# Cross-attention and feed-forward, one core: x loaded ahead of the high halves' transposition, its statistics in two parts

## The chip, the core and the metric

The kernel runs on one core of a Trainium2 chip. The metric is the device time of one execution in microseconds (us), the median of several runs. The core has a matrix engine (TensorE, PE in the profile), VectorE (DVE), ScalarE (ACT), GpSimd (POOL) and SyncE (SP), which here issues every DMA. The engines run their own instruction lists in order and meet at semaphores: an instruction whose semaphore has not reached its value holds everything behind it on its engine. That holds for SyncE too: a DMA that waits keeps back all DMAs behind it.

## What is computed

A block of 16 batches with 512 tokens of width 512: attention over 120 context rows with rotary positions (16 heads of 32), and a gated feed-forward (512 to 1536 to 512) whose tensors are quantised and dequantised by their largest value.

```
x = x + xattn(layernorm(x), ctx, ctx, Wq, Wk, Wv, Wo)
x = x + ffn(layernorm(x), w_gate, w_up, w_down)

# xattn: rope on q and k, softmax of q k^T / sqrt(32), times v, times Wo
# ffn:   x, up, gate, gate*sigmoid(gate) and the product are rounded to
#        16 bit levels of their largest value, weights to 4 bit in blocks of 32
```

## The kernel before

It has four stages one after the other: attention for all batches (to about 740 us), then the gate, the up and the down projection, each bound by TensorE. Only the attention stage is touched.

**Steps.** Attention is cut into units, one per batch and quarter of the heads: 4 x 16 = 64 units `u`. A loop over steps `s` (0 to 66) is written out on each engine (`sp_attention`, `pe_attention`, `act_attention`, `dve_attention`, `pool_attention`), with `b, c = divmod(s, 4)`, and each step works on several units at different depths. In a middle step TensorE does, in this order: the scores of unit s-7 (line 668, then the maxima's part, 675), the queries of unit s (693), the scores from which the row maxima are taken, of unit s-2 (716), the output projection of an old unit (752), every fourth step (c = 2) the transposition of the maxima (726), and the values and sums of unit s-7 (771, 776). All scores use the same four banks of PSUM, so the scores of line 668 wait for VectorE's maxima (line 1341) of the step before, and the scores of line 716 wait for ScalarE's exponentials (line 975).

**Queries.** ScalarE copies the queries of unit s out of PSUM (998). The rotation needs neighbouring rows swapped: SyncE does this with two DMAs (`sp_swap`, lines 398 and 399, tile QW). GpSimd multiplies with the cosine (1471) and, when the swap has landed, the sine (1480); VectorE adds the two in the next step (`dve_rope_add`, 1139), ahead of the maxima of unit s-2 on its list.

**x of a batch.** One tile X (XA[0]) holds x of one batch at a time. Which step does what for batch nb is set by `x_at(s, part)`, which is true for s = 4 nb - 5 + part (for nb from 3 on):
- `sp_x_load` (424): 1 MB from memory into X, in step 4 nb - 6 (c = 2), behind the transposition of the batch before. It waits for s_xlo, that is until VectorE has computed the low halves of the batch before out of X.
- `dve_x_stats` (1149, 1154), step 4 nb - 5 (c = 3): four sums (BN_STATS) and their means, at the end of the step's list. GpSimd makes the deviations from them (`pool_deviation`, 1488 and 1490, a power), VectorE the shift (`dve_x_shift`, 1160) and ScalarE the normalised x (933), step 4 nb - 4 (c = 0).
- `act_x_high` and `dve_x_low` (946, 1169), step 4 nb - 3 (c = 1): x is split into a high and a low half of 16 bit (ST).
- `sp_x_turn` (433): each half is transposed by a DMA into XD, the high one in step 4 nb - 3 (c = 1), the low one in the next (c = 2). The queries of batch nb begin in step 4 nb.

So in a step with c = 1 SyncE issues the high transposition of batch nb, in the next the low one and then the load of batch nb + 1.

**Also in the row.** On SyncE stand in every step the write of x1 (x plus attention) of one unit (465), the load of its next x row (480), and the two swaps; in c = 0 and 1 two loads each of reciprocal rows (445, tile RB) which GpSimd multiplies into the attention output (1505) before ScalarE's copies (1018); in c = 3 the sums are written out and read back (451, 455), in c = 0 the reciprocals go out (459). VectorE begins each step with x1 of a unit and its statistics (1191, 1203, 1208, 1209), and every fourth step has a part of the feed-forward weights' preparation (1244 to 1264).

Of the kernel before, what the change touches and what calls it, by code (L numbers as in the profile page):

```python
# [13 lines left out]
B, S, D, NH, SK, F = 16, 512, 512, 16, 120, 1536  # L14
# [31 lines left out]
def kv_at(s):  # L46

    first = sum(n for t, n in KV_STEPS.items() if t < s)
    return range(first, first + KV_STEPS.get(s, 0))
# [16 lines left out]
def normal_at(s):  # L66

    b, c = divmod(s - 13, 4)
    return [4 * b + 2 * c, 4 * b + 2 * c + 1] if 0 <= b < B - 2 and c < 2 else []


def output_at(s):

    if s < 16:
        return []
    return [s - 16] if s < NU + 1 else [[LATE - 1, LATE], [LATE + 1], [LATE + 2]][s - NU - 1]
# [7 lines left out]
def x_at(s, part):  # L84

    for b in range(2, B):
        if s == 4 * b - 5 + part + (b == 2):
            return [b]
    return []


def w_step(k):

    return 16 + 4 * k


def build(nc, x, ctxt, wq, wk, wv, wo, w_gate, w_up, w_down, cosq, sinq, cosk, sink, eye, out, scr):
    x1_d, g_d, gq_d, up_d, xt_d, wt_d, sr_d = scr
    stack = ExitStack()
    with stack:  # L100
# [269 lines left out]
        def w_home(k):  # L370
            return wt_d[k // 12, k % 12]

        def x1_rows(b):
            return x[b].rearrange("(p j) d -> p j d", j=4)
# [18 lines left out]
        def sp_swap(e, n, w):  # L393

            e.wait_ge(s_qe, n + 1)
            if n >= 2:
                e.wait_ge(s_radd, n - 1)
            e.dma_start(QW[n % 2][0:128:2, 0:w], qe(n)[1:128:2, 0:w]).then_inc(s_qw[n % 2], 16)
            e.dma_start(QW[n % 2][1:128:2, 0:w], qe(n)[0:128:2, 0:w]).then_inc(s_qw[n % 2], 16)

        def sp_ctx_load(e, g):
            if g == 1:
                e.wait_ge(s_clo, 1)
            elif g == 2:
                e.wait_ge(s_wlo, 1)
            elif g == 3:
                e.wait_ge(s_am, AMAX.index("ctx1") + 1)
                e.wait_ge(s_tp, 4)
            e.dma_start(CX[g][0:SK], ctxt[4 * g:4 * g + 4].rearrange("b s d -> s b d")).then_inc(CXS[g][0], 16)
# [11 lines left out]
        def sp_x_load(e, b):  # L421
            if b:
                e.wait_ge(s_xlo, 2 * b)
            e.dma_start(X[:], x1_rows(b)).then_inc(s_x, 16)
# [32 lines left out]
        def dma_recip_out(e, b):  # L457
            e.wait_ge(s_rr, rr(b))
            e.dma_start(sr_d[1 + b % 2].rearrange("r (e f) -> (r e) f", f=64), RG[:]).then_inc(s_rd, 16)

        def sp_x1_out(e, u):

            _, x1, i, _ = x_of(u)
            e.wait_ge(s_x1, u + 1)
            e.dma_start(x1_d[u // 4, :, u % 4, :], x1).then_inc(s_x1d[i], 16)
# [25 lines left out]
        def sp_attention(e):  # L491
            e.dma_start(id32[:], eye).then_inc(s_id, 16)
            sp_ctx_load(e, 0)
            e.dma_start(WLD[0], wk.rearrange("(k p) e -> p k e", p=128)).then_inc(s_wld[0], 16)
            sp_x_load(e, 0)
            for a, t in ((ck, cosk), (sk, sink)):
                e.dma_start(a, t).then_inc(s_tab, 16)
            e.dma_start(WLD[1], wq.rearrange("(k p) e -> p k e", p=128)).then_inc(s_wld[1], 16)
            for a, t in ((cq[:], cosq), (sq[:], sinq)):
                e.dma_start(a, t).then_inc(s_tab, 16)  # L500
            e.dma_start(WLD[2], wv.rearrange("(k p) e -> p k e", p=128)).then_inc(s_wld[2], 16)
            sp_ctx_load(e, 1)
            sp_ctx_load(e, 2)
            for n in range(4):
                sp_swap(e, n, 4 * SK)
            sp_x_load(e, 1)
            for s in range(NSTEP):
                b, c = divmod(s, 4)

                for u in output_at(s - 1):  # L510
                    sp_x1_out(e, u)
                for u in output_at(s + 1):
                    sp_xr_load(e, u)

                if c == 0 and 0 <= b - 3 < B - 1:
                    dma_recip_out(e, b - 3)
                if s < NU:
                    sp_swap(e, ROT["q", s], 512)
                for i in kv_at(s):
                    if i % 8 < 4:  # L520
                        sp_swap(e, ROT["k", i], 4 * SK)

                for u in normal_at(s + 1):
                    dma_recip(e, u)

                if c == 3 and 0 <= b - 2 < B - 1:
                    dma_sums_out(e, b - 2)
                    dma_sums_in(e, b - 2)
                if s == 1:
                    sp_ctx_load(e, 3)  # L530
                if s == 4:
                    sp_ctx_turn(e, 2)
                if s == 6:
                    sp_ctx_turn(e, 3)
                if s == 9:
                    e.wait_ge(s_v, 12)
                    e.dma_start(WLD[3], wo.rearrange("(k p) e -> p k e", p=128)).then_inc(s_wld[3], 16)

                for nb in [1] if s == 2 else x_at(s, 2):
                    sp_x_turn(e, nb, 0)  # L540
                    if s < 16:
                        sp_x_turn(e, nb, 1)
                for nb in x_at(s - 1, 2) if s > 16 else []:
                    sp_x_turn(e, nb, 1)
                if c == 2 and 2 <= b + 2 < B:
                    sp_x_load(e, b + 2)

                for k in range(12):
                    if w_step(k) == s:
                        if k == 0:  # L550
                            e.wait_ge(s_v, 16)
                        if k >= 2:
                            e.wait_ge(s_wl, k - 1)
                        e.dma_start(w_ld[k % 2], w_source(k)).then_inc(s_ld[k % 2], 16)
                    if w_step(k) + 6 == s:
                        e.wait_ge(s_wl, k + 1)
                        e.dma_start(w_home(k), w_hl).then_inc(s_ws, 16)
                if s >= 57:
                    sp_gate_turn(e, s - 57)

                if s == 64:
                    for i in range(2):
                        if i == 0:
                            e.wait_ge(s_xlo, 2 * B)
                        else:
                            e.wait_ge(s_xt, 32 * (B - 1))
                        e.wait_ge(s_x1d[0], 32 * (i + 1))
                        e.wait_ge(s_x1d[1], 32 * (i + 1))
                        e.dma_start(XA[i][:], x1_d[i]).then_inc(s_xl[i], 16)

            dma_sums_out(e, B - 2)
            sp_x1_out(e, LATE + 1)
            sp_xr_load(e, LATE + 3)
            sp_xr_load(e, LATE + 4)
            dma_sums_in(e, B - 2)
            sp_x1_out(e, LATE + 2)
            sp_xr_load(e, LATE + 5)
            dma_recip_out(e, B - 2)
            for u in range(NU - 8, NU - 4):
                dma_recip(e, u)  # L580
            sp_x1_out(e, LATE + 3)
            sp_xr_load(e, LATE + 6)
            for u in range(LATE + 4, NU):
                sp_x1_out(e, u)
                if u + 3 < NU:
                    sp_xr_load(e, u + 3)
                if u == NU - 4:
                    sp_gate_turn(e, NO - 2)
                    sp_gate_turn(e, NO - 1)
# [551 lines left out]
                g, r = divmod(i, 8)  # L1141
                e.tensor_tensor(KR[g][:, r, :], KR[g][:, r, :], QW[n % 2][:, 0:4 * SK], ALU.add).then_inc(s_radd, 1)

        def dve_x_stats(e, b):
            e.wait_ge(s_x, 16 * (b + 1))
            if b >= 2:
                e.wait_ge(s_lmv, b - 1)
            for j in range(4):
                e.bn_stats(st1[b % 2][:, j, :], X[:, j, :]).then_inc(s_lst, 1)
            e.wait_ge(s_lst, 4 * b + 4)  # L1150
            if b >= 2:
                e.wait_ge(s_lnb, b - 1)
            for j in range(4):
                t = e.bn_aggr(mv1[b % 2][:, j, :], st1[b % 2][:, j, :])
            t.then_inc(s_lmv, 1)

        def dve_x_shift(e, b):
            q = rs1[b % 2]
            e.wait_ge(s_lrs, 2 * b + 2)
            e.scalar_tensor_tensor(q[:, 4:8], mv1[b % 2][:, :, 0], -1.0, q[:, 0:4], ALU.mult, ALU.mult).then_inc(s_lnb, 1)  # L1160
# [105 lines left out]
        def dve_attention(e):  # L1266
# [35 lines left out]
            for s in range(NSTEP):  # L1302
                b, c = divmod(s, 4)
# [11 lines left out]
                    dve_x_stats(e, 1)  # L1315
                if s == 1:
                    dve_x_shift(e, 1)
                if 1 <= s <= NU:
                    dve_rope_add(e, ROT["q", s - 1])
                    for i in kv_at(s - 1):  # L1320
                        if i % 8 < 4:
                            dve_rope_add(e, ROT["k", i])
# [1083 lines left out]
```

## Time and profile before

| | us |
|---|---|
| median of 3 runs | 2319.28 (2317.97 to 2320.76) |
| profiled execution | 2318.47 |
| its span in the trace | 2316.7 |
| TensorE busy | 2199.2 (95%) |
| VectorE busy | 1686.2 (73%) |
| ScalarE busy | 1330.6 (57%) |
| GpSimd busy | 704.9 (30%) |

Shares of the whole span say little here, since attention and the feed-forward have different limits. From 400 to 500 us, in the middle of attention, TensorE is busy 94.2 us, VectorE 89.6, ScalarE 63.0 and GpSimd 69.7, the DMA engines at a share of 0.80, and TensorE's clock is granted in full. A step takes about 9 to 10 us, a batch about 38.

A row of a timeline gives the start in us, the time it took, engine, line, operation, the tiles it writes and reads, how many instructions were merged in it, and in brackets how long the engine was idle before it and what ended that. In steps 37 to 41 the first scores of TensorE (line 668) start at 433.71, 442.56, 452.59, 461.74 and 472.47; what VectorE does for a step runs a little behind that. Times in the text are those of this trace.

### The profile page before, as it was taken

What the parts mean: (1) busy time and instruction counts of PE and PEld (TensorE: products, weight loads), DVE (VectorE), ACT (ScalarE), POOL (GpSimd) and SP (SyncE); (2) the same over time, 40 slices, a digit from 0 to 9 for tenths busy, and PEclk for the clock granted to TensorE, in tenths of its full rate; (3) what the DMA queues carried; (4) which work ended last, traced back from release to release, by engine and by line L of the source; (5) the groups of instructions that cost most, each with busy time, mean ns of one, the idle gap of its engine ahead of it and who ended that gap; (6) DMA issues with size and microseconds to landing.
All of it is one profiled execution on the core that took longest, in us unless ns stands there. A gap on an engine that the chain in (4) does not pass through costs nothing. (4 is left out here: it accounts for less than half of the span.)

```text
span 2316.7 us, 31161 instructions
## 1 busy us (share of the span) xinstructions
PE 2199.2 (95%) x12037; PEld 970.5 (42%) x12037; DVE 1686.2 (73%) x1690; ACT 1330.6 (57%) x1299; POOL 704.9 (30%) x655
## 2 busy tenths in 40 slices
PE   5898999999988899999999999999998799999999
PEld 3443333333332444444444444444443344444444
DVE  7656899898975766445543598888888887778773
ACT  3345666666644232222322787877877777777772
POOL 3444675766663311000100364444444000000000
PEclk9899999999999999999999999999999899999999
DMA  6334686877777568888875898877876565655552
GB/s 193 95 103 116 179 194 173 193 173 192 170 159 178 164 215 256 272 246 253 250 227 180 292 329 311 299 286 286 293 284 259 189 234 211 236 226 205 205 217 91
DMA packets 287190, 500.14 MB, mean 216 GB/s; under 512 B 187980, under 2 KB 190284, under 8 KB 250172
## 3 DMA queue, kind: packets, MB, share of 16 engines
q1 hardware_dynamic: 287036, 498.10, 68.1%
q8 instruction: 95, 1.56, 0.3%
q14 instruction: 59, 0.48, 0.1%
HBM read 247.75 MB, written 186.58 MB: 187 GB/s over the span
## 5 line engine op out<-in xcount | busy, mean ns | idle before, releaser
L1698 PE MATMUL banks<-XB,W 128*128 128x512 f16 x2304 | 500.1, 380 | 2.3 <-ACT XB L1724 2.3
L1698 PE MATMUL banks<-XB,WT 128*128 128x512 f16 x2304 | 497.4, 379 | 0.0
L2164 PE MATMUL banks<-W,OH 128*128 128x512 f16 x2256 | 487.1, 379 | 3.6 <-DVE OH L2266 3.6
L1718 ACT ACTIVATE OB<-banks,uns 128x512 f32<-128x512 f32 x384 | 255.7, 684 | 393.2 <-PE banks L1698 390.4
L1698 PEld LDWEIGHTS banks<-XB,W 128*128 128x128 f16 x2304 | 225.9, 98 | 276.1 <-issue 5.1
L1698 PEld LDWEIGHTS banks<-XB,WT 128*128 128x128 f16 x2304 | 225.4, 98 | 271.8
L2164 PEld LDWEIGHTS banks<-W,OH 128*128 128x128 f16 x2256 | 220.7, 98 | 270.0 <-DVE OH L2266 4.0
L1985 POOL TENSOR_TENSOR PR<-GS,OB 128x2048 f32<-128x2048 f32 x46 | 220.5, 4794 | 257.6 <-ACT OB L1718 247.6
L1807 DVE TENSOR_REDUCE amx<-OB 128x1 f32<-128x2048 f32 x48 | 109.7, 2285 | 239.8 <-ACT OB L1718 239.8
L752 PE MATMUL banks<-XC,AH 128*128 128x512 f16 x768 | 179.2, 385 | 5.4 <-POOL AH L1510 3.7
L693 PE MATMUL banks<-XD,WQ 128*128 128x512 f16 x768 | 177.0, 380 | 2.2 <-ACT WQ L878 0.8
L975 ACT ACTIVATE P<-banks 120x2048 f32<-120x2048 f32 x60 | 112.3, 1872 | 86.5 <-PE banks L675 86.5
L1341 DVE TENSOR_REDUCE MX<-banks 128x16 f32<-128x1920 f32 x64 | 137.6, 2149 | 25.2 <-PE banks L716 25.2
L1949 DVE TENSOR_REDUCE amf<-PR 128x4 f32<-128x2048 f32 x47 | 107.4, 2286 | 52.5 <-POOL PR L1985 52.1
L2227 ACT ACTIVATE OH<-OQ 128x2048 f16<-128x2048 int16 x47 | 89.5, 1904 | 93.7 <-DVE OQ L2261 92.7
L2289 DVE SCALAR_TENSOR_TENSOR Y<-banks,gm,XRd 128x512 f32<-128x512 f32 x64 | 46.3, 745 | 116.5 <-PE banks L2164 116.5
L1480 POOL TENSOR_TENSOR QW<-QW,sq 128x512 f32<-128x512 f32 x64 | 90.3, 1411 | 130.6 <-DMA QW<-QE 129.9
L2247 DVE SCALAR_TENSOR_TENSOR GSd<-SQd,XD 128x2048 f32<-128x2048 int32 x47 | 107.6, 2289 | 15.2 <-ACT SQd L2209 15.2
L693 PEld LDWEIGHTS banks<-XD,WQ 128*128 128x128 f16 x768 | 70.1, 98 | 113.4 <-issue 33.6
L1931 DVE SCALAR_TENSOR_TENSOR GS<-SQ,GQ 128x2048 f32<-128x2048 int32 x48 | 109.5, 2282 | 9.8 <-ACT SQ L1906 9.8
L1933 DVE TENSOR_REDUCE amg<-GS 128x1 f32<-128x2048 f32 x48 | 109.7, 2286 | 1.7
L2261 DVE SCALAR_TENSOR_TENSOR OQ<-AQ,gm,BQ 128x2048 int16<-128x2048 int16 x47 | 110.1, 2342 | 0.9 <-ACT AQ L2215 0.9
(272 smaller groups left out, 2866.2 us busy)
## 6 DMA issues: line engine op xcount, KB each, us to landing
g_s<-OB SPq DMA_DIRECT2D x48, 1024.0 KB, 6.0
GL<-g_s SPq DMA_DIRECT2D x48, 1024.0 KB, 7.3
up_s<-OB SPq DMA_DIRECT2D x48, 1024.0 KB, 4.9
XA<-up_s SPq DMA_DIRECT2D x32, 1024.0 KB, 9.3
gq_s<-GQ SPq DMA_DIRECT2D x48, 512.0 KB, 4.7
XD<-gq_s SPq DMA_DIRECT2D x48, 512.0 KB, 6.7
XA<-in_x SPq DMA_DIRECT2D x16, 1024.0 KB, 6.3
QW<-QE SPq DMA_DIRECT2D x128, 128.0 KB, 3.0
```

The costliest lines, as they stand in the source:

```text
L693: t = e.matmul(BQ_.rearrange("p (j t) -> p j t", j=4), WQ[:, a, k, c * 128:(c + 1) * 128], XT[b % 2][:, xa, :, k, :], start=(n == 0 and k ...
L752: t = e.matmul(o_bank(u), AH[b % 2][:, a, k, j * 128:(j + 1) * 128], WO[:, wa, k, :], start=(n == 0), stop=(n == 11))
L975: e.activation(P[0:SK], PB[0:SK, 0:4, :], ACT.Exp, scale=SM_SCALE).then_inc(s_p, 1)
L1341: e.tensor_reduce(MX[mb % 2][:, :, :, mc].rearrange("p j g -> p g j"), PB[:, 0:4, 0:4 * SK].rearrange("p g (j s) -> p g j s", j=4), AX.X, ...
L1698: t = e.matmul(pk[:].rearrange("p (j t) -> p j t", j=4), WT[w][:, ot, wa, kk, :], XB[i % 2][:, xa, :, kk, :], start=(kk == 0 and wa == 0 a ...
L1718: e.activation(OB[n % 3][:, r, :], bank[(k + 4) % 8][:], ACT.Copy, scale=uns[:, 12 * w + ot:12 * w + ot + 1]).then_inc(s_ev, 1)
L1807: e.tensor_reduce(amx[:, m:m + 1], flat(OB[m % 3][:]), AX.X, ALU.max, apply_absolute_value=True).then_inc(s_gr, 1)
L1931: e.scalar_tensor_tensor(GS[m % 2][:], SQ[m % 2][:], 65535.0, GQ[m % 2][:], ALU.min, ALU.mult).then_inc(s_gs, 1)
L1933: e.tensor_reduce(amg[:, m:m + 1], GS[m % 2][:], AX.X, ALU.max, apply_absolute_value=True).then_inc(s_gsm, 1)
L1985: e.tensor_tensor(PR[:], GS[m % 2][:].rearrange("p (a t) -> p a t", a=4), OB[(NC + m) % 3][:], ALU.mult).then_inc(s_pr, 1)
L2164: t = e.matmul(pk[:].rearrange("p (r n) -> p r n", r=4), OH[i % 2][:, a, ot, j * 128:(j + 1) * 128], WD[:, :, c, wa, o4, :], start=(ot == ...
L2261: e.scalar_tensor_tensor(OQ[m % 2][:], AQ[m % 2][:], gm[:, 10:11], BQ[m % 2][:], ALU.mult, ALU.mult).then_inc(s_doq, 1)
```

## The change

On SyncE, from step 16 on, the load of x moves from step 4 nb - 6 (c = 2, behind the low halves' transposition of batch nb - 1) to step 4 nb - 7 (c = 1, ahead of its high halves' transposition). It concerns batches 6 to 15. Its wait for s_xlo is unchanged and now stands ahead of the transposition's waits.

On VectorE the function `dve_x_stats` is split. For batches 6 to 15 the sums of the first two quarters are taken by `dve_x_sums(e, nb, 0)` in the same step (c = 3), but behind x1's statistics and ahead of the addition on the queries; the other two sums and the means stay where all four were.

```
+                if s >= 16 and c == 1 and b + 2 < B:
+                    sp_x_load(e, b + 2)
                 for nb in [1] if s == 2 else x_at(s, 2):
                     sp_x_turn(e, nb, 0)
                     if s < 16:
                         sp_x_turn(e, nb, 1)
                 for nb in x_at(s - 1, 2) if s > 16 else []:
                     sp_x_turn(e, nb, 1)
-                if c == 2 and 2 <= b + 2 < B:
+                if s < 16 and c == 2:
                     sp_x_load(e, b + 2)
...
-        def dve_x_stats(e, b):
+        def dve_x_sums(e, b, part):
+
             e.wait_ge(s_x, 16 * (b + 1))
             if b >= 2:
                 e.wait_ge(s_lmv, b - 1)
-            for j in range(4):
+            for j in range(2 * part, 2 * part + 2):
                 e.bn_stats(st1[b % 2][:, j, :], X[:, j, :]).then_inc(s_lst, 1)
+
+        def dve_x_stats(e, b):
+            if b < 6:
+                dve_x_sums(e, b, 0)
+            dve_x_sums(e, b, 1)
             e.wait_ge(s_lst, 4 * b + 4)
...
                 if s == 1:
                     dve_x_shift(e, 1)
+                for nb in x_at(s, 0) if s >= 16 else []:
+                    dve_x_sums(e, nb, 0)
                 if 1 <= s <= NU:
                     dve_rope_add(e, ROT["q", s - 1])
```

SyncE in a step with c = 1 and the next, before (line 433 is a transposition, 465 x1 out, 480 an x row in, 398 and 399 the swap, 424 the load of x):

```order
185 L433 DMA_TRANSPOSE XD<-XA 128x16x128
186 L465 DMA x_s<-RX 128x512
187 L480 DMA RX<-in_x 128x512
188 L398 DMA QW<-QE 64x512
189 L399 DMA QW<-QE 64x512
190 L433 DMA_TRANSPOSE XD<-XA 128x16x128
191 L424 DMA XA<-in_x 128x2048
192 L557 DMA wt_s<-RW 128x1024
193 L465 DMA x_s<-RX 128x512
```

and after the change:

```order
185 L424 DMA XA<-in_x 128x2048
186 L433 DMA_TRANSPOSE XD<-XA 128x16x128
187 L465 DMA x_s<-RX 128x512
188 L480 DMA RX<-in_x 128x512
189 L398 DMA QW<-QE 64x512
190 L399 DMA QW<-QE 64x512
191 L433 DMA_TRANSPOSE XD<-XA 128x16x128
192 L559 DMA wt_s<-RW 128x1024
193 L465 DMA x_s<-RX 128x512
```

The load has moved past both transpositions, x1's two transfers and one swap.

VectorE in a step with c = 3, before (the row of x1's statistics, the addition on the queries, the maxima, the sums of x, their means, and x1 of the next step):

```order
150 L1209 TENSOR_REDUCE xmn<-RX 128x1
151 L1139 TENSOR_TENSOR QR<-QR,QW 128x512
152 L1341 TENSOR_REDUCE MX<-banks 128x4x4
153 L1149 BN_STATS st<-XA 128x6 x4
154 L1154 BN_AGGR mv<-st 128x2 x4
155 L1191 SCALAR_TENSOR_TENSOR RX<-banks,vun,RX 128x512
```

and after (lines 1141, 1351, 1152, 1162 and 1199 are what 1139, 1341, 1149, 1154 and 1191 were):

```order
150 L1217 TENSOR_REDUCE xmn<-RX 128x1
151 L1152 BN_STATS st<-XA 128x6 x2
152 L1141 TENSOR_TENSOR QR<-QR,QW 128x512
153 L1351 TENSOR_REDUCE MX<-banks 128x4x4
154 L1152 BN_STATS st<-XA 128x6 x2
155 L1162 BN_AGGR mv<-st 128x2 x4
```

Two of the four sums have moved ahead of the addition and the maxima; the rest keeps its order.

## Rows read from the trace of the kernel before

**Rows 1.** Waits of TensorE, 340 to 640: us in total, times, longest.

```profile
PE banks L668 <- DVE MX L1341: 10.1, 9, 1.8
PE banks L716 <- ACT P L975: 6.1, 12, 0.8
```

**Rows 2.** Timeline of TensorE, steps 37 to 41.

```profile
433.71 1.13 PE L668 MATMUL banks<-QR,W 32*120 32x512 f32 x8 [1.40 <-DVE MX L1341]
...
447.29 0.39 PE L716 MATMUL banks<-W,QE 32*128 32x120 f16 x16 [0.68 <-ACT P L975]
...
461.74 1.13 PE L668 MATMUL banks<-QR,W 32*120 32x512 f32 x8
...
465.72 0.39 PE L716 MATMUL banks<-W,QE 32*128 32x120 f16 x16
...
472.47 1.13 PE L668 MATMUL banks<-QR,W 32*120 32x512 f32 x8 [1.81 <-DVE MX L1341]
```

**Rows 3.** Timeline of VectorE, steps 39 and 40.

```profile
456.77 1.63 DVE L1139 TENSOR_TENSOR QR<-QR,QW 128x512 f32<-128x512 f32 x1 [0.94 <-POOL QW L1480]
458.32 2.15 DVE L1341 TENSOR_REDUCE MX<-banks 128x16 f32<-128x1920 f32 x1
462.19 2.47 DVE L1149 BATCH_NORM_STATS2 st<-XA 128x6 f32<-128x512 f32 x4 [1.72 <-DMA XA<-in_x]
...
470.27 2.14 DVE L1341 TENSOR_REDUCE MX<-banks 128x16 f32<-128x1920 f32 x1
```

**Rows 4.** Timeline of SyncE, steps 36 to 40.

```profile
433.23 1.25 SPq L445 DMA_DIRECT2D RB<-sr_s  x2
...
444.81 5.20 SPq L433 DMA_TRANSPOSE XD<-XA  x1
...
451.22 0.53 SPq L398 DMA_DIRECT2D QW<-QE  x1
...
455.51 0.85 SPq L424 DMA_DIRECT2D XA<-in_x  x1
...
470.33 1.25 SPq L445 DMA_DIRECT2D RB<-sr_s  x2
```

**Rows 5.** DMA issues, 340 to 640: count, KB each, median us from issue to landing.

```profile
XA<-in_x SPq DMA_DIRECT2D x8, 1024.0 KB, 6.4
```

**Rows 6.** DMA issues, about 451.8: the swap of step 38.

```profile
QW<-QE SPq DMA_DIRECT2D x2, 128.0 KB, 3.5
```

**Rows 7.** DMA issues, about 459.1: the swap of step 39.

```profile
QW<-QE SPq DMA_DIRECT2D x2, 128.0 KB, 6.4
```

**Rows 8.** DMA issues, 444.5 to 445.5: the high halves' transposition, us to landing.

```profile
XD<-XA SPq DMA_TRANSPOSE x1, 8.0
```

**Rows 9.** Timeline of GpSimd, steps 38 and 39.

```profile
455.47 1.27 POOL L1480 TENSOR_TENSOR QW<-QW,sq 128x512 f32<-128x512 f32 x1
...
466.13 1.27 POOL L1480 TENSOR_TENSOR QW<-QW,sq 128x512 f32<-128x512 f32 x1 [5.47 <-DMA QW<-QE]
...
467.76 1.32 POOL L1490 TENSOR_TENSOR rs<-rs,mh 128x4 f32<-128x4 f32 x1
```

**Rows 10.** Timelines of TensorE, VectorE and SyncE in an early batch, step 17.

```profile
247.14 1.13 PE L668 MATMUL banks<-QR,W 32*120 32x512 f32 x8
...
254.01 4.30 DVE L1169 TENSOR_TENSOR XA<-XA 128x1024 f16<-128x1024 f32 x2 [0.30 <-ACT XA L946]
...
255.74 5.77 SPq L433 DMA_TRANSPOSE XD<-XA  x1
...
262.70 0.52 SPq L398 DMA_DIRECT2D QW<-QE  x1
```

**Rows 11.** Stretches: their length, busy us of each engine, clock, DMA share, GB/s.

```profile
444.00:446.00 2.00, 2.00 (x10) 0.88 (x9) 1.52 (x3) 1.88 (x3) 2.00 (x3) 1.00 0.27 99
446.00:448.00 2.00, 1.32 (x21) 0.56 (x20) 1.42 (x1) 1.28 (x2) 2.00 (x3) 1.00 2.01 151
...
457.00:462.00 5.00, 5.00 (x48) 1.86 (x44) 3.47 (x2) 2.08 (x5) 3.66 (x3) 1.00 0.91 262
```

More of the change, by code:

```diff
@@ L537, in sp_attention @@
                     e.dma_start(WLD[3], wo.rearrange("(k p) e -> p k e", p=128)).then_inc(s_wld[3], 16)
+                if s >= 16 and c == 1 and b + 2 < B:
+                    sp_x_load(e, b + 2)
                 for nb in [1] if s == 2 else x_at(s, 2):
@@ L544, in sp_attention @@
                     sp_x_turn(e, nb, 1)
-                if c == 2 and 2 <= b + 2 < B:
+                if s < 16 and c == 2:
                     sp_x_load(e, b + 2)
@@ L1142, in dve_rope_add, with dve_x_sums @@
                 e.tensor_tensor(KR[g][:, r, :], KR[g][:, r, :], QW[n % 2][:, 0:4 * SK], ALU.add).then_inc(s_radd, 1)
-        def dve_x_stats(e, b):
+        def dve_x_sums(e, b, part):
             e.wait_ge(s_x, 16 * (b + 1))
@@ L1147, in dve_x_stats @@
                 e.wait_ge(s_lmv, b - 1)
-            for j in range(4):
+            for j in range(2 * part, 2 * part + 2):
                 e.bn_stats(st1[b % 2][:, j, :], X[:, j, :]).then_inc(s_lst, 1)
+        def dve_x_stats(e, b):
+            if b < 6:
+                dve_x_sums(e, b, 0)
+            dve_x_sums(e, b, 1)
             e.wait_ge(s_lst, 4 * b + 4)
@@ L1317, in dve_attention @@
                     dve_x_shift(e, 1)
+                for nb in x_at(s, 0) if s >= 16 else []:
+                    dve_x_sums(e, nb, 0)
                 if 1 <= s <= NU:
```

## The prediction, made before the changed kernel ran

> **What bounds the kernel now.** I read the views in the order of the groups. First the waits of TensorE between 340 and 640 us: nearly all its holes are 10.1 us before the scores, on the score maxima of VectorE (9 times), and 6.1 us on the exponentials of ScalarE (12 times) [rows 1]. So this stretch is bound by TensorE with some 16 us of holes, and the change can't give more than that. Its timeline shows where the first kind lies: the scores of step 41 start at 472.47 after 1.81 us of waiting, those of step 37 at 433.71 after 1.40, those of step 40 at 461.74 without [rows 2]. Eight of the nine are in steps with s mod 4 = 1, once a batch; the first two of the ten batches that the change touches have none. The ninth is a short one, and I leave it in.
>
> Next, who makes VectorE late there. Its timeline in steps 39 and 40: it ends the maxima of step 39 at 460.47, stands idle 1.72 us until x has landed, takes the four sums from 462.19 to 464.66, then the means, x1 with its statistics, the addition on the queries, reciprocal and shift, and only at 470.27 the maxima of step 40 [rows 3], though TensorE had written their scores at 466.11 [rows 2]. Behind that lies the queue of SyncE: x is issued at 455.51 [rows 4] and takes 6.4 us in the median to land [rows 5]. The swap of the queries behind it takes 6.4 us too, where that of the step before took 3.5 [rows 6, 7]. GpSimd therefore stands idle 5.47 us before the sine product of step 39 [rows 9].
>
> **The change part by part.** The work is the same: four sums of 2.47/4 = 0.62 us, one x load and two transpositions a batch. Batches 6 to 15 are touched, ten in all, and only places change.
>
> The load goes from behind the low halves' transposition (step 38) to before the high halves' (step 37), some ten us earlier: the 1.72 us of waiting go. Two of the sums (1.24 us) go ahead of the addition on the queries, where VectorE was idle 0.94 us from 455.83 on [rows 3]: that addition starts at 455.83 + 1.24 = 457.07, 0.30 late. The maxima of step 39 end at 460.77, the other two sums at 462.0 instead of 464.66: 2.7 us earlier. The swap of step 39 has no load ahead of it; issued at 459.1 and given the 3.5 us of rows 6, it lands at 462.6, the sine product (1.27 us) ends near 463.9, the power for the deviations (1.32 us) near 465.5 [rows 9]. So GpSimd does not hold VectorE there, and its maxima of step 40, 2.7 us ahead at most, wait for the scores at 466.11: they run from some 467.6 at the latest to 469.7. TensorE wants them at 470.66 (472.47 less 1.81). The wait goes: **-10.1 us**, bounds 0 and -10.1.
>
> What is late next is the swap of step 38, behind the load, the high transposition, x1 and its x row. It landed at 451.8 + 3.5 = 455.3 [rows 6], just when GpSimd was free for it (sine product at 455.47 [rows 9]). VectorE's addition waits for that product; the maxima behind it end at 460.47 and TensorE wants them at 461.74 [rows 2, 3]: 1.27 us of slack, of which the sums take 0.30, so 1.0 is left. How late will the swap be? Issuing the load takes 0.6 of SyncE (0.59 in most of its rows; the one shown has 0.85 [rows 4]). For the load's bytes the trace has no plain load ahead of a transposition here. While SyncE issues the transposition (5.20 us [rows 4]) the engines move 99 GB/s at a busy share of 0.27; under the load they move 262 [rows 11]. If it fits into that gap, (262 - 99) GB/s x 5.2 us = 0.85 of its 1.05 MB go there, and 0.20 MB, 0.8 us, are left. If nothing fits, as the busy share of 2.01 from 446 to 448 [rows 11] may mean, it costs 1.05 MB / 262 GB/s = 4.0 us. I take 0.8, as SyncE's 5.2 us of issuing look like what sets the pace: delay 1.4 us, of which 0.4 reaches TensorE, ten times: **+4.0 us**; bounds 0 and 10 x (4.6 - 1.0) = +36.
>
> The Trainium skill speaks against this choice: Advanced Engine Details and Errata, section X-Bar Transpose (TRN2), says that transposing transfers run as fast as regular ones. There would be no gap then, the load would push the swap by its full 4.0 us and the sum would be a loss. The trace disagrees so far: 512 KB of transposition take 8.0 us to land, 1024 KB of load 6.4 [rows 5, 8].
>
> The load also waits for the low halves of the batch before (s_xlo), and behind it on SyncE stand the transposition and the swap. In the early batch VectorE computes the low halves until 254.01 + 4.30 = 258.31 and SyncE is ready at 255.74: 2.57 us of new waiting [rows 10]; in 5 of the ten batches SyncE comes first in this way. There, however, the swap was issued 15.6 us behind the scores of the step before (262.70 - 247.14 [rows 10], the scores of step 17 and the swap of step 18), against 451.22 - 433.71 = 17.5 around 444 [rows 2, 4], so such a batch only gets to where the others are. I price it at nothing; bound 1 us for each of the five. The transposed halves are wanted in step 40 only, x1's rows a step later: over 5 us of cover.
>
> Last, the waits on the exponentials. At 447.29 TensorE waits 0.68 [rows 2] since ScalarE's copies wait for GpSimd's product, and that for the reciprocals' rows, issued at 433.23 [rows 4], 0.48 us before the scores of step 37. Where they were issued 2.14 ahead (470.33 against 472.47 [rows 2, 4]) this wait is absent. Five of the 12 are of this kind, 3.4 us. With reciprocal and swap 2 us earlier the rows go out near 468.2, 2.4 us ahead of 470.66: these waits should go. I count half, **-1.7 us**, bounds 0 and -6.1.
>
> Sum: -10.1 + 4.0 - 1.7 = -7.8 us. The profiled execution took 2318.47 (span 2316.7, 1.8 around it) and becomes 2310.7; the median of the runs is 0.8 higher, so 2319.28 - 7.8 = **2311.5 us**. Everything behind 740 us is the same instructions.
>
> **The rivals.** *The collision only moves* (2319). The wait of step 41 goes and one as long comes at the scores of step 40. For it: the swap of step 38 has no slack at GpSimd, and the load waits in half of the batches. Against: the 99 GB/s under the transposition. With the swap 2.2 us late, 10 x (2.2 - 1.0) = 12 us eat the 11.8 gained.
>
> *Slower* (2328). Same place, one mechanism: the load's bytes do not fit into the transposition, and the swap of step 38 lands 3 us or more late. Price: 10 x (3.0 - 1.0) - 11.8 = +8.2, so 2327.5; it decides from 2.2 us of delay on. Rows 6 and 7 show the mechanism at today's place, 2.9 us between a swap behind the load and one that is not. The first two batches, with no wait to win, pay first. The Trainium skill, DMA: Bandwidth & Descriptors, section Queues, rings and completion order, has each engine take its descriptors in ring order; by that rule every byte of the load stands before the swap.
>
> *All holes close* (2303). The swap is late by under 1 us and both kinds of wait go: -10.1 - 6.1 = -16.2. For it: the first two batches run without the first kind. Against: the maxima of step 39 keep but 1.0 us of slack.
>
> **How the numbers follow.** Forecast 2311.5 (its own range 2307 to 2316): 0.45. Moved collision: 0.25. Slower: 0.18. All holes: 0.12. The range leaves out the upper half of the slower case and the end of the last: 2303.0 to 2325.0. About 0.2%, 4.6 us, is what a measurement of this kernel can tell from no change. Faster (below 2314.6) takes the first case but for its edge and the last: 0.54; same 0.27; slower (above 2323.9) 0.19.
>
> **What would show it.** Right: no idle VectorE before the sums, no wait at the scores of s mod 4 = 1; the swap of s mod 4 = 3 landing in about 3.5 us, and GpSimd's 5.47 us of idling gone; at s mod 4 = 0 waits of 0 to 0.6 us. Wrong: TensorE waiting 1 us or more on the maxima at s mod 4 = 0, GpSimd idle before the sine product of s mod 4 = 2, SyncE standing at the load for the low halves with everything behind it late. If TensorE's holes hardly shrink though the wait for x is gone, the error is in the 0.8 us.

## The result, and the profile after

| | before | after |
|---|---|---|
| median of 9 runs each | 2319.28 us (2316.29 to 2326.7) | 2331.57 us (2325.08 to 2334.59) |
| profiled execution | 2318.47 | 2331.95 |
| its span | 2316.7 | 2330.1 |

The changed kernel takes 1.0046 times as long, 95% interval 1.0032 to 1.006. That is 12.3 us more, where 7.8 less was forecast; the time lies above the range as well. The sign and the place are those of the rival called *Slower*, and the loss is larger than its 8.2 us. Some kernels of the experiments had one execution that was far longer than the rest (2381 to 11083 us); the ratios leave it out, the medians count it, which moves them by up to 1.3 us.

First the waits of TensorE after the change, 340 to 640 us (us in total, times, longest); they answer to [rows 1].

```profile
PE banks L670 <- DVE MX L1351: 13.5, 8, 3.0
PE banks L718 <- ACT P L977: 5.4, 9, 0.8
```

The wait for the score maxima has grown from 10.1 to 13.5 us. Its place has changed completely: over 240 to 640 there are ten such waits, 17.6 us, and all ten are at the scores of steps with s mod 4 = 0, one a batch; at s mod 4 = 1 there is none left. The timeline of TensorE in the batch with one of the largest, steps s mod 4 = 3, 0 and 1:

```profile
421.39 1.13 PE L670 MATMUL banks<-QR,W 32*120 32x512 f32 x8
...
433.49 2.08 PE L670 MATMUL banks<-QR,W 32*120 32x512 f32 x8 [2.88 <-DVE MX L1351]
...
443.83 1.14 PE L670 MATMUL banks<-QR,W 32*120 32x512 f32 x8
```

Who is late? VectorE, the same stretch; the row with 3.92 is the addition on the queries, and the first row the two sums that the change moved:

```profile
424.54 1.28 DVE L1152 BATCH_NORM_STATS2 st<-XA 128x6 f32<-128x512 f32 x2
429.73 1.63 DVE L1141 TENSOR_TENSOR QR<-QR,QW 128x512 f32<-128x512 f32 x1 [3.92 <-POOL QW L1490]
431.28 2.15 DVE L1351 TENSOR_REDUCE MX<-banks 128x16 f32<-128x1920 f32 x1
433.35 1.27 DVE L1152 BATCH_NORM_STATS2 st<-XA 128x6 f32<-128x512 f32 x2
```

The sums no longer wait for x: the 1.72 us of [rows 3] are gone. But the addition waits 3.92 us for GpSimd's sine product, where it waited 0.94. GpSimd in turn waited for the swap, and the swap of the next step arrives promptly:

```profile
428.42 1.28 POOL L1490 TENSOR_TENSOR QW<-QW,sq 128x512 f32<-128x512 f32 x1 [4.21 <-DMA QW<-QE]
...
434.33 1.27 POOL L1490 TENSOR_TENSOR QW<-QW,sq 128x512 f32<-128x512 f32 x1 [0.74 <-DMA QW<-QE]
```

And behind the swap lies SyncE, from the load of x on (step s mod 4 = 1) to the swap of step s mod 4 = 3:

```profile
413.59 0.47 SPq L424 DMA_DIRECT2D XA<-in_x  x1
414.17 8.30 SPq L433 DMA_TRANSPOSE XD<-XA  x1
...
423.66 0.52 SPq L398 DMA_DIRECT2D QW<-QE  x1
424.23 1.12 SPq L399 DMA_DIRECT2D QW<-QE  x1
425.45 3.12 SPq L433 DMA_TRANSPOSE XD<-XA  x1
...
430.78 0.62 SPq L399 DMA_DIRECT2D QW<-QE  x1
```

This is the row to look at. SyncE stands at the high transposition for 8.30 us, against 5.20 in [rows 4]. Everything behind it on SyncE is late by that, and so is the swap, whose own transfer has not become slower: the DMA issues around 413.6 to 414.5 and at 423.7 (us to landing) show it.

```profile
XA<-in_x SPq DMA_DIRECT2D x1, 1024.0 KB, 9.3
...
XD<-XA SPq DMA_TRANSPOSE x1, 11.9
```

```profile
QW<-QE SPq DMA_DIRECT2D x2, 128.0 KB, 3.6
```

**All ten batches.** I took the same instants in each, counted from the scores of the step with s mod 4 = 1 (the means of ten, 240 to 660 us; the trace of each kernel's profiled execution):

| us | before | after |
|---|---|---|
| high transposition starts on SyncE | 10.0 | 11.1 |
| SyncE stands at it | 5.5 | 7.6 |
| swap of s mod 4 = 2 has landed | 21.45 | 24.3 |
| scores of s mod 4 = 0 | 27.8 | 29.4 |
| from there to the next s mod 4 = 1 | 10.0 | 9.65 |
| whole batch | 37.8 | 39.1 |

Ten batches are 12.8 us longer, which is the loss within its noise. It is +16.3 up to the scores of s mod 4 = 0 and -3.5 behind them. Behind the landing stand the sine product 1.28, the addition 1.63 and the maxima 2.15, 5.1 us together; 24.3 + 5.1 = 29.4, so after the change this chain ends last in the mean of the batches. Before, 21.45 + 5.1 = 26.6 left 1.2 us of slack. The delay is 2.85 us, and 10 x (2.85 - 1.2) = 16.5.

### The profile page after: what moved, and what is told of

Its sections match the earlier page's. It is cut to its first block and busy times, and to the rows that moved or that the text cites. A ratio compares the mean times of both kernels' runs of the same rounds, so it can differ in the third digit from the quotient of the medians.

```text
span 2330.1 us, 31175 instructions
## 1 busy us (share of the span) xinstructions
PE 2206.6 (95%) x12037; PEld 972.2 (42%) x12037; DVE 1679.0 (72%) x1690; ACT 1328.1 (57%) x1299; POOL 704.1 (30%) x655
## 5 line engine op out<-in xcount | busy, mean ns | idle before, releaser
L695 PE MATMUL banks<-XD,WQ 128*128 128x512 f16 x768 | 182.0, 388 | 2.3 <-ACT WQ L880 0.8
```

The source lines that it names most:

```text
L695: t = e.matmul(BQ_.rearrange("p (j t) -> p j t", j=4), WQ[:, a, k, c * 128:(c + 1) * 128], XT[b % 2][:, xa, :, k, :], start=(n == 0 and k ...
```

## The experiments

Each edit is against the changed kernel, except where it is said; ratios are to the kernel before. "Stands at it" is SyncE's time at the high transposition and "landed" the instant of the table above, both as means of ten batches.

### The four sums left together

If the split of the sums were to blame, leaving them together would bring the time back. The load is moved as in the change; the sums stand where they were.

```
         def dve_x_stats(e, b):
-            if b < 6:
-                dve_x_sums(e, b, 0)
+            dve_x_sums(e, b, 0)
             dve_x_sums(e, b, 1)
...
-                for nb in x_at(s, 0) if s >= 16 else []:
-                    dve_x_sums(e, nb, 0)
```

> Only the load of x is moved ahead of the high halves' transposition; the four sums stay together behind the maxima. Theory 1 (the load's bytes hold up the transposition, SyncE stays 8 us instead of 5 in its issue, and the swap of s mod 4 = 2 lands some 4 us late): as slow as the whole change, ratio to before 1.003 to 1.008, waits of TensorE at the scores of s mod 4 = 0 still 1 to 3 us in most batches, since the two sums lay in VectorE's idle time. Theory 2 (the two sums ahead of the addition on the queries make the maxima late): ratio 0.997 or less, and waits at s mod 4 = 0 under 0.5 us.

Measured: 2330.82 us, ratio 1.0055 (1.004 to 1.0071). The split is not to blame; the moved load alone makes the loss.

### The same instructions with fewer bytes

The rest of the change is kept, with its wait for the low halves, but the load of batches 6 to 15 brings a quarter or a half of x, so that the other parts of the tile keep old values.

```
-            e.dma_start(X[:], x1_rows(b)).then_inc(s_x, 16)
+            if b >= 6:
+                e.dma_start(X[:, 0:1, :], x1_rows(b)[:, 0:1, :]).then_inc(s_x, 16)
+            else:
+                e.dma_start(X[:], x1_rows(b)).then_inc(s_x, 16)
```

> The change with a load that brings only one of four parts of x for batches 6 to 15 (256 KB instead of 1024; the other three parts keep old values, so this leaves out three quarters of the loads). Place, issue and the wait for the low halves are unchanged. Theory 1 (bytes): the transposition's issue goes back to about 5 us, the swap of s mod 4 = 2 is late by 1 to 2 us, TensorE's waits at s mod 4 = 0 fall from 17.6 us in all to under 6, ratio to before 0.994 to 0.998. Theory 3 (SyncE standing at the load for the low halves, 10.2 us in all, makes the swap late): waits stay at 10 us or more, ratio 1.001 or more.

The half (`0:2` in place of `0:1`):

> The change with a load of only the first two of four parts (512 KB; leaves out half of x for batches 6 to 15). It sets the dose between 256 KB (ratio 0.994) and 1024 KB (1.005). If the delay of the swap grows with the bytes and only what exceeds about 1 us of slack reaches TensorE: swap 1.5 to 2.5 us late, waits at s mod 4 = 0 between 2 and 9 us in all, ratio 0.996 to 1.000. If there is a fixed cost of any larger load there, 1.003 or more.

Measured, with the changed kernel beside them:

| load | time us | ratio | landed |
|---|---|---|---|
| 256 KB | 2304.23 | 0.9944 (0.993 to 0.9957) | 21.4 |
| 512 KB | 2307.78 | 0.9959 (0.9944 to 0.9973) | 22.3 |
| 1024 KB, the change | 2331.57 | 1.0046 (1.0032 to 1.006) | 24.3 |

SyncE with 256 KB, the rows that answer to 413.59 to 424.23 above:

```profile
402.00 0.34 SPq L425 DMA_DIRECT2D XA<-in_x  x1
402.44 5.07 SPq L436 DMA_TRANSPOSE XD<-XA  x1
...
408.71 0.52 SPq L398 DMA_DIRECT2D QW<-QE  x1
```

With a quarter of the bytes SyncE stands at the transposition for 4.7 us in the mean, with all of them 7.6: 2.9 more, and the swap lands 2.9 later. In both the transposition starts 11.1 us behind the scores, so the load's place, its issue and its wait for the low halves are the same, and in the kernel with 256 KB they cost nothing: its swap lands at 21.4, as before the change. SyncE does wait for the low halves, eight times in the changed kernel (the line below, 240 to 640 us), and nine times, 14.7 us, in this one, which is the fastest of all:

```profile
SPq L424 <- DVE XA L1177: 10.2, 8, 2.7
```

TensorE's wait for the maxima is as good as gone with 256 KB (240 to 640):

```profile
PE banks L721 <- ACT P L980: 4.0, 7, 0.8
PE banks L673 <- DVE MX L1354: 0.2, 1, 0.2
```

So the bytes ahead of the transposition are what makes the swap late. From 256 to 1024 KB are 0.79 MB, and at the 262 GB/s of [rows 11] that is 3.0 us; the landing moves by 2.9. So each byte beyond the first quarter is paid in full, as if nothing of it went under the transposition. The time follows with a threshold, since up to 1.2 us of delay there is slack: 22.3 is still within it, 24.3 is not. These two kernels also move less in all; the next ones don't.

### The same bytes behind the high transposition

The load is issued in the same step, directly behind the transposition instead of ahead of it.

```
-                if s >= 16 and c == 1 and b + 2 < B:
-                    sp_x_load(e, b + 2)
                 for nb in [1] if s == 2 else x_at(s, 2):
                     sp_x_turn(e, nb, 0)
                     if s < 16:
                         sp_x_turn(e, nb, 1)
+                if s >= 16 and c == 1 and b + 2 < B:
+                    sp_x_load(e, b + 2)
```

> The change, but with the load issued directly behind the high halves' transposition instead of ahead of it, still ahead of x1's two transfers and the swap of s mod 4 = 2. Theory A (bytes simply add: whatever stands ahead of the swap delays it by 1 MB / 262 GB/s = 4 us): same as the change, ratio 1.003 to 1.007, waits at s mod 4 = 0 of 14 to 20 us in all. Theory B (a load ahead of a transposition is worse than one behind it, since the transposition's issue on SyncE then grows from 5 to 8 us and holds all that is behind): the issue is back at 5 us, the swap is issued 3 us earlier, and the ratio is 0.997 to 1.002.

Measured: 2316.45 us, ratio 0.9992 (0.9981 to 1.0002), no difference to the kernel before. SyncE in one batch:

```profile
410.64 5.05 SPq L433 DMA_TRANSPOSE XD<-XA  x1
415.73 0.57 SPq L424 DMA_DIRECT2D XA<-in_x  x1
...
418.59 0.59 SPq L399 DMA_DIRECT2D QW<-QE  x1
```

SyncE's time at the transposition is back at 5.5 in the mean. Issued at 17.8 (before 17.4), the swap lands at 23.5: now its bytes stand behind the load's and need 5.7 us instead of 4.0. By the chain 23.5 + 5.1 = 28.6, and the scores of s mod 4 = 0 come 28.6 behind those of s mod 4 = 1. Ahead of the transposition the load costs the swap 2.85 us, behind it 2.1.

### The load between the swap and the low transposition

One place further, in step s mod 4 = 2 behind the swap, with the four sums together (the edit on SyncE is shown against the kernel before):

```
+                if s >= 16 and c == 2 and b + 2 < B:
+                    sp_x_load(e, b + 2)
                 for nb in x_at(s - 1, 2) if s > 16 else []:
                     sp_x_turn(e, nb, 1)
```

> The load stands between the swap of s mod 4 = 2 and the low halves' transposition; sums together as before the change. Its wait for the low halves is long fulfilled there. Theory 1: the swap of this step is as early as before, x lands about 3 us earlier than before, the low transposition's issue grows by some 3 us and pushes the swap of s mod 4 = 3 as today's load does; the waits at s mod 4 = 1 shrink or stay, none comes at s mod 4 = 0; ratio 0.996 to 1.001. If every load ahead of any transposition costs (bytes plus something of the transposition's own), 1.002 or more.

Measured: 2321.11 us, ratio 1.0009 (0.9999 to 1.002), no difference. The swap lands at 21.0, so nothing is lost at s mod 4 = 0 by it. TensorE's waits for the maxima fall from 10.1 to 5.7 us (six), but those on the exponentials rise from 6.7 to 9.2 (eleven; all over 240 to 640). Moving the whole load past one transposition gains 4.4 us on the one wait and gives 2.5 of them back on the other; what is left is too little for the medians.

### Another queue

The load is issued by ScalarE, behind its exponentials of step s mod 4 = 2, and SyncE has none:

```
+                if s >= 16 and c == 2 and b + 2 < B:
+                    sp_x_load(e, b + 2)
                 if 0 <= u < NU:
```

> The change's sums in two parts, but the load is issued by ScalarE in the step with s mod 4 = 2, behind the exponentials, so that it stands in no row of SyncE and its wait for the low halves is over. If what hurts is the order within SyncE's queue (theory 1 in its narrow form): SyncE's swap of s mod 4 = 2 is issued as early as before and lands up to 1.5 us late at most, the waits at s mod 4 = 1 go, ratio 0.993 to 0.998. If it is the load's bytes on the 16 engines, whoever issues them (theory 1 in its wide form): the load still shares the time of the transposition and the swap still lands 2 us or more late, ratio 1.000 to 1.005.

Measured: 2387.35 us, ratio 1.0317 (1.0296 to 1.0338), far worse than either theory allowed. The DMA issues of 245 to 640, us to landing in the median:

```profile
XA<-in_x ACTq DMA_DIRECT2D x9, 1024.0 KB, 14.4
XD<-XA SPq DMA_TRANSPOSE x18, 14.3
```

Load and transposition from two queues take 14 us each, where from one they take 8.0 and 7.9 after the change. ScalarE issues the load 10.9 us behind the scores of s mod 4 = 1, some 2.5 us behind the start of the high transposition, so both are under way together; SyncE stands at the high transposition for 6.4 us, at the low one for 9.5 (3.1 after the change), and the swap lands at 27.5. TensorE's wait for the maxima becomes 49.5 us in nine waits of up to 9.9. The Trainium skill, DMA: Bandwidth & Descriptors, section Queues, rings and completion order, says that each DMA engine takes turns between the queues it has work for, a packet at a time. No run here shows these turns; why both transfers take nearly twice as long, and which of them holds back which, is not settled.

### The load in parts

Four kernels cut the load in pieces, each with its own wait at the sums that need it (first two quarters, last two quarters). The edit is the same but for the places:

```
+        def sp_x_part(e, b, j0, j1, sem_):
+            e.wait_ge(s_xlo, 2 * b)
+            e.dma_start(X[:, j0:j1, :], x1_rows(b)[:, j0:j1, :]).then_inc(sem_, 16)
```

*A half ahead of the high transposition, a half behind the low one (the load's old place):*

> All of x is loaded, in two DMAs: the first two parts ahead of the high halves' transposition, the other two where the load stood before the change; the sums of the first half are taken ahead of the addition, those of the second behind the maxima. By the bytes: each of the two swaps is held up by half a load, waits at s mod 4 = 0 as in the half-bytes run (2 to 9 us), those at s mod 4 = 1 mostly gone; ratio 0.996 to 1.001. If the time is set by the sum of bytes a batch and not by where they stand: 1.000 to 1.005.

*A quarter ahead of each transposition, a half behind the low one:*

> All of x in three DMAs: a quarter ahead of the high halves' transposition, a quarter ahead of the low one (behind the swap), a half where the load stood before; sums in two parts as in the change. By the bytes the quarter ahead of the high one costs nothing (as in the quarter-bytes run), the rest holds up the swap of s mod 4 = 3, which has about 2 us of slack: waits of TensorE on the maxima under 4 us in all, ratio 0.994 to 0.998. If x's last half still lands after the maxima (VectorE waiting for x again), 0.998 to 1.001.

*A half ahead of the high transposition, a half between the swap and the low one:*

> All of x in two halves: the first ahead of the high halves' transposition, the second between the swap of s mod 4 = 2 and the low halves' transposition; sums in two parts. By bytes: the swap of s mod 4 = 2 lands as in the half-bytes run (22 to 23 us behind the scores of s mod 4 = 1), the low transposition takes about 4 us to issue instead of 3, the swap of the next step lands by 30, x is there for both sums. Waits on the maxima 1 to 6 us in all, ratio 0.995 to 0.999. If all bytes a batch count alike, 0.9985 as with the half behind the low transposition.

*A half behind the high transposition, a half between the swap and the low one:*

```
                 for nb in [1] if s == 2 else x_at(s, 2):
                     sp_x_turn(e, nb, 0)
...
+                if s >= 16 and c == 1 and b + 2 < B:
+                    sp_x_part(e, b + 2, 0, 2, s_xa)
+                if s >= 16 and c == 2 and b + 2 < B:
+                    sp_x_part(e, b + 2, 2, 4, s_x)
                 for nb in x_at(s - 1, 2) if s > 16 else []:
                     sp_x_turn(e, nb, 1)
```

> As the run before, but with the first half behind the high halves' transposition instead of ahead of it, ahead of x1's transfers. If ahead or behind makes a difference by itself, as 1024 KB seemed to show (1.0046 and 0.9992), this is 0.001 to 0.003 below the run before; if at half the bytes the slack takes it up, the two are equal within their intervals. Its load does not stand waiting for the low halves, as those are ready when the transposition is issued.

| places of the parts | time us | ratio | TensorE on the maxima, on the exponentials, 240 to 640 |
|---|---|---|---|
| half ahead of high, half in the old place | 2314.0 | 0.9988 (0.9977 to 0.9999) | 6.7 and 7.5 us |
| quarter, quarter, half | 2314.46 | 0.9986 (0.9973 to 0.9998) | 6.0 and 7.6 |
| half ahead of high, half between | 2316.56 | 0.9986 (0.9973 to 0.9999) | 5.2 and 10.7 |
| half behind high, half between | 2307.08 | 0.9952 (0.9937 to 0.9967) | 0.4 and 6.9 |

The first three are hardly faster than the kernel before; for the one in quarters more had been expected. Most of their waits on the maxima are again at s mod 4 = 1: what is late there is the swap of s mod 4 = 3, which lands at 30.7 to 30.9 in the mean of ten batches (before 31.0, in the last kernel 29.3). The last is 11 us faster with all bytes loaded. Its waits of TensorE:

```profile
PE banks L725 <- ACT P L984: 6.9, 11, 0.8
PE banks L677 <- DVE MX L1361: 0.4, 1, 0.4
```

The swap of s mod 4 = 2 lands at 22.15 and x is there in time. Against the whole load behind the transposition (2316.45) it has only half of the bytes ahead of the swap; against the third row of the table it has that half behind the high transposition and not ahead of it. Both differences were worth some 9 us. The second isn't one of bytes under the transposition: SyncE stands at it for 5.5 us in the third kernel and 5.3 in the last. But in the third the load waits for the low halves ahead of it (14.4 us in eight waits over 240 to 640, none in the last), and the transposition starts at 11.9 and not at 9.9. Whether this wait or the order makes the 9 us is not separated; with 256 KB in all, a wait as long had cost nothing.

### Both transpositions behind the swap

If the transposition's hold on SyncE is what delays the swap, the load may stand at s mod 4 = 1 as in the change once the transposition has left that place. The high one goes to s mod 4 = 2, next to the low one.

```
-                for nb in [1] if s == 2 else x_at(s, 2):
+                for nb in [1] if s == 2 else x_at(s, 2) if s < 16 else []:
                     sp_x_turn(e, nb, 0)
-                    if s < 16:
-                        sp_x_turn(e, nb, 1)
+                    sp_x_turn(e, nb, 1)
                 for nb in x_at(s - 1, 2) if s > 16 else []:
+                    sp_x_turn(e, nb, 0)
                     sp_x_turn(e, nb, 1)
```

> The change, but both transpositions stand behind the swap of s mod 4 = 2, so that the load has step s mod 4 = 1 for itself. If only bytes and issue ahead of the swaps count: the swap of s mod 4 = 2 lands at 19 to 21 us behind the scores of s mod 4 = 1 and the wait at s mod 4 = 0 is gone; the two transpositions in a row hold the swap of s mod 4 = 3 to about 30, just in time, and the transposed halves land 1 to 2 us ahead of the queries; ratio 0.994 to 0.998. If they land behind the queries' start, TensorE waits there for XD and the ratio is 1.000 or more.

Measured: 2308.08 us, ratio 0.9956 (0.9941 to 0.9971). SyncE (the last row holds both transpositions):

```profile
404.84 0.47 SPq L424 DMA_DIRECT2D XA<-in_x  x1
...
409.65 0.60 SPq L399 DMA_DIRECT2D QW<-QE  x1
410.34 7.33 SPq L433 DMA_TRANSPOSE XD<-XA  x2
```

The swap is issued 4.8 us behind the load instead of 10.6, ahead of the transpositions' hold, and lands at 20.9 in the mean. This and the last kernel in halves are the two versions with all of x loaded that are clearly faster than both kernels, by the same 10 to 11 us against the kernel before within their intervals.

### TensorE's clock

After the change TensorE's clock is granted at 0.57 of full speed from 433 to 437, right behind the hole of 2.88 us, and in full before it (columns as in [rows 11]):

```profile
427.00:431.50 4.50, 3.60 (x25) 1.01 (x22) 1.77 (x2) 0.15 (x2) 3.08 (x3) 1.00 1.18 230
433.00:437.00 4.00, 3.52 (x16) 1.18 (x17) 3.93 (x11) 0.97 (x1) 3.06 (x4) 0.57 0.24 81
```

The level is the lower one, 1.2 GHz instead of 2.4: the eight score products take 2.08 us in place of 1.13. The changed kernel has five such episodes of about 3.4 us in 240 to 660, the kernel before none; each follows a hole at s mod 4 = 0, and the step then lasts 10.3 to 10.5 us instead of 8.85. The five come to 8.0 us. Are they a part of the loss? To see it, unused products were put into the holes; their result is read by nobody:

```
+                if c == 0 and 20 <= s <= 56:
+                    e.wait_ge(s_qe, ROT["q", s - 1] + 1)
+                    for k in range(6):
+                        e.matmul(BQ_, WQ[:, 0, k % 4, 0:128], WQ[:, 0, k % 4, :], start=True, stop=True)
                 if 0 <= s - 7 < NU:
                     pe_scores(e, s - 7)
```

> The whole change, with six extra products on TensorE (128x128 by 512, some 0.23 us each, results unused) ahead of the scores of the ten steps with s mod 4 = 0 from 20 to 56, where TensorE stood idle 0.6 to 3.0 us. Theory C (part of the loss is TensorE's clock: the five times 3.4 us at half clock behind the longest of these holes, about 1.6 us each, 8 us in all): the episodes are gone or down to one or two; the products lengthen only the four short holes, by 2 to 3 us in all; ratio to before 1.0005 to 1.003, faster than the change at 1.0046. Theory D (the clock has no part, the waits explain it all): ratio 1.005 to 1.007.

Measured: 2328.62 us, ratio 1.0044 (1.0028 to 1.006), as slow as the change and between the two theories. The episodes are gone (the window from 240 to 640 has 1.00 where the change has 0.98), and half of the hole is filled, the scores behind it at full speed:

```profile
240.00:640.00 400.00, 385.30 (x2910) 145.44 (x2903) 353.27 (x503) 248.07 (x340) 259.09 (x212) 1.00 0.73 176
```

```profile
431.36 1.47 PE L812 MATMUL banks<-WQ 128*128 128x512 f16 x6
...
433.95 1.13 PE L670 MATMUL banks<-QR,W 32*120 32x512 f32 x8 [1.12 <-DVE MX L1355]
```

From the scores of s mod 4 = 0 to the next ones it now takes 8.86 us in the mean, 8 us less over ten. But the way from s mod 4 = 1 to 0 has grown from 29.4 to 30.0, and the batch is 38.85 us against 39.06. The swap still lands where SyncE's queue lets it, some 24.8 behind the scores, and in eight of the ten batches the scores come within 0.1 us of the landing and the chain behind it; in the other two the unused products themselves were in the way, 1.1 us together. So giving TensorE its clock back gained 2 us of the 8 in the traces and nothing that the medians can tell (the profiled execution of this kernel, 2336.12, was its slowest and lost time elsewhere; only the stretch is compared). The kernel with the sums left together has three episodes instead of five and is as slow, though it differs by the sums as well. So the 8 us can't be taken as a term of their own in the 12.3. Why the landing moved back by half a microsecond with the clock at full speed is open; 0.2 of it is a later start of the high transposition (11.3 against 11.1).

## Why the prediction was wrong

**The bytes that don't fit: the step that failed.** The sum gave the delay of the swap as 0.6 for the load's issue and 0.8 for bytes that don't fit under the transposition, 1.4 us. It measured 2.85. Against the kernel before, SyncE starts the transposition 1.1 us later and stands at it 2.1 us longer; against the kernel with 256 KB, which has the same start and no delay, it is the longer stand alone (2.9). The working took [rows 11], 99 GB/s at a busy share of 0.27 while SyncE issues a transposition, as a gap that other bytes may use. That row covers 2 us, of which 0.8 lie ahead of the issue. Over the whole of SyncE's stand at the transposition, before and after (columns as in [rows 11]), there is no such gap:

```profile
444.80:450.00 5.20, 4.52 (x37) 1.96 (x36) 4.14 (x4) 4.20 (x6) 5.03 (x6) 1.00 0.94 115
```

```profile
414.20:422.50 8.30, 7.62 (x66) 3.07 (x64) 7.04 (x11) 4.83 (x7) 8.13 (x8) 1.00 1.04 185
```

Before the change the 16 engines are already busy at a share of 0.94, at only 115 GB/s; a low rate was read as idle time. (The view books a whole packet where it starts, so that short stretches show 0.27 here and 2.01 there, and a share can stand above 1.) After it 1.5 MB go in 8.3 us where 0.6 went in 5.2: 0.9 MB more in 3.1 us. SyncE's 5.2 us are no pace of their own either: with 1 MB queued ahead the stand is 7.6 us in the mean, with 256 KB 4.7. The bytes of the last three quarters were paid in full, and about the first quarter's time was hidden. The delay of 2.85 lies between the 1.4 taken and the 4.6 of the bound.

The Trainium skill (Advanced Engine Details and Errata, X-Bar Transpose (TRN2)) has transposing transfers as fast as regular ones, and the prediction said that by this rule the delay would be the full 4.0 us. The loss was rightly to be feared, but the traces don't agree with the rule itself: in the kernel before 512 KB of transposition take 6.7 us to land in the median (240 to 640), 1024 KB of load 6.4, and during SyncE's stand the engines move 115 GB/s, against 262 under the load.

**The sum, term by term.** From 7.8 us less to 12.3 more are 20.1 us. The swap's delay makes 12.5 of them (+16.5 for +4.0), the gain at s mod 4 = 1 that did not come 6.6 (-3.5 for -10.1); the 1.0 that is left is of the size by which the waits on the exponentials fell short (-0.7 for -1.7), and less than the medians can tell. With the delay alone put right the sum would have been 4.7 us more than before, so the second term failed as well; it is taken up below.

**The slack and the multiplication held.** 1.0 us of slack was read from one batch, 1.2 is the mean of ten. With a delay of 2.85 in place of 1.4 and this slack the term becomes +16.5 instead of +4.0, and +16.3 was measured.

**The wait for x went, as said; its 10.1 us did not all come.** No wait of TensorE at s mod 4 = 1 is left, VectorE is not idle before the sums. Yet the way from the scores of s mod 4 = 0 to the next became only 0.35 us shorter, 3.5 over the ten, since the five half-clock episodes fall into just this step. Without them it is 1.14 shorter, which is the 10.1 and a little more, but then the other part grows, as the filled holes show. The term was booked as if it stood by itself; that the swap's chain takes the gain back is what the traces of the filled kernel suggest, and no run shows it by itself. The rival *Slower* had the mechanism and its 3 us right (2.85). It booked a gain of 11.8 where 3.5 came, and a price of 20 where 16.3 did; so it was 4 us short of the loss.

**The swap of s mod 4 = 3** lands in 3.4 us, GpSimd's 5.47 us of [rows 9] before its sine product are 0.74, as forecast.

**The low halves' wait** was priced at nothing with a bound of 1 us for five batches. There are eight such waits, 10.2 us. That they cost nothing is shown for the quarter load, with nine waits and 14.7 us. Here the term held. Between the last two kernels in halves such a wait may be what differs, so it can't be carried over as nothing.

**The waits on the exponentials** were to lose 1.7 us. Over 340 to 640 they fell from 6.1 to 5.4 us, 0.7. Small, and right in its sign; the batches being longer, nothing can be made of it.

**The choice of the likeliest.** Four cases were laid out by the delay of one transfer, and the point from which the sign turns, 2.2 us, was right: the kernel with half the bytes and the one with the load behind the transposition, with delays of 0.9 and 2.1 us, come out faster and the same, the change with 2.85 slower. The chance of 0.18 for the side beyond it was too small for a term whose bounds were 0 and 4.6 and whose low end rested on one reading of a gap.

## What to carry to other kernels

A transposing DMA was not a short instruction here for the engine that issues it: it held SyncE for 5.5 us, all that stood behind it on SyncE waited, and 1 MB ahead of it made that 7.6. So before a load is moved ahead on a shared queue, look for the small, urgent transfer that comes next behind the two, and take its slack as the budget. Where that was too little, two orders helped in this kernel: the load in halves on either side of the urgent transfer, the first behind the transposition (0.9952), and the transposition behind the urgent transfer (0.9956); the whole load behind the urgent one gained nothing (1.0009). Where a row shows a low rate, read the busy share over the whole of the transfer before calling it a gap.

## What the runs showed of the hardware that was not expected

- SyncE's stand at a transposition of 512 KB depends on what was queued ahead of it: 4.7 us with a 256 KB load, 5.45 with 512 KB, 7.6 with 1024 KB, some 0.7 to 1.1 us for each further 256 KB. With none it is 5.5, but there the transposition starts 1.1 us earlier; by when SyncE is free again, counted from the scores of s mod 4 = 1, it is 15.5 us with none, 15.8, 16.7 and 18.7.
- During that stand the 16 DMA engines are busy at a share of 0.94 while they move 115 GB/s (one batch of the kernel before).
- A 1 MB load from ScalarE's queue next to transpositions from SyncE's: 14.4 and 14.3 us to landing, against 8.0 and 7.9 from one queue.
- Five holes of TensorE of 1.79 to 3.03 us were followed by some 3.4 us at half clock; behind one of 1.74, and behind those of the kernel before, up to 1.81, there was none. Filling the holes ended the episodes and made the kernel no faster.
